# A planned Mamba and mixture-of-experts layer: ScalarE's side work cut into single activations, routing products into pieces, and new written-out orders

## The reference, cut to what matters

```python
xz = einsum('bld,ed->bel', x, in_proj_w);  x, z = halves           # 1024 channels each
x = silu(conv4(x) + conv_b)                                        # four taps along time
dt_lo, B, C = split(einsum('bdl,kd->blk', x, x_proj_w))
delta = softplus(dt_lo @ dt_proj_w.T + dt_proj_b)
h_t = h_(t-1) * exp(delta_t * A) + delta_t * B_t * x_t             # 16 states a channel
y = (sum over states of h * C + D * x) * silu(z);  out = y @ out_proj_w.T
x1 = layernorm(x + out)
w = softmax(top 2 of x1 @ gate_w.T)
x2 = layernorm(x1 + sum over the two experts of w * (x1 @ expert_w.T + expert_b))
```

## Time and profile before

| what | value |
|---|---|
| median of three runs | 2285.7 us (2283.76 to 2297.6) |
| span of the profiled execution | 2281.1 us |
| busy share of the span | PE 89%, DVE 87%, POOL 81%, ACT 73% |
| mean granted clock of PE | 0.941 of full speed |

### The profile page before, as it was taken

The page is one execution under the profiler, slowest core; times in us unless marked ns, Lnnn a source line. Parts: engine busy times, 40 slices in busy tenths (PEclk is TensorE's granted clock), DMA queues, the critical chain, the costliest instruction groups (busy, mean ns, idle before and its releaser), DMA issues.

```text
span 2281.1 us, 30428 instructions
## 1 busy us (share of the span) xinstructions
PE 2037.1 (89%) x8624; PEld 1201.8 (53%) x8624; DVE 1983.3 (87%) x2191; ACT 1660.2 (73%) x3074; POOL 1850.8 (81%) x1505
## 2 busy tenths in 40 slices
PE   8896779789898989999899989999799998879998
PEld 3444455455554645545555555645455555545543
DVE  5899999899999989898899899899898988889911
ACT  5758858677598856988588876989579785666534
POOL 2959999589898979889898889899898897686503
PEclk9896879889999999999999999999999999769999
DMA  5513143158854776557754687556855575466875
GB/s 169 180 47 92 38 139 111 51 172 252 278 129 143 241 255 180 143 168 257 256 152 119 201 266 234 129 180 216 284 149 141 180 252 209 123 209 215 278 278 120
DMA packets 222085, 412.79 MB, mean 181 GB/s; under 512 B 29880, under 2 KB 36152, under 8 KB 221920
## 3 DMA queue, kind: packets, MB, share of 16 engines
q1 hardware_dynamic: 180448, 322.36, 42.1%
q0 software_dynamic: 20496, 57.16, 12.3%
q10 hardware_dynamic: 20976, 31.33, 4.1%
HBM read 299.37 MB, written 85.72 MB: 169 GB/s over the span
## 4 chain that ended last, share of the span: by engine, by line
POOL 25%; PE 10%; issue 9%; DMA 7%; DVE 7%; ACT 3%; SPq 1%; ACTq 0%; DVEq 0%; POOLq 0%
POOL hst L1704 12%; PE bank L1137 8%; POOL first_dbu L1704 4%; DMA y<-scaled 2%; DVE hst L1755 2%; DVE y L1744 2%; POOL delta L1675 2%; POOL u L1678 2%; DVE hst L1920 1%; DMA Bbc<-b_scratch 1%; POOL ysb L1630 1%; DVE u L1775 1%; PE hTp L1153 1%; POOL zs L1649 1%; ACT dA L1563 1%
## 5 line engine op out<-in xcount | busy, mean ns | idle before, releaser
L1563 ACT ACTIVATE dA<-delta,negA 128x512 f32<-128x512 f32 (+1 forms) x1146 | 712.2, 636 | 307.9 <-DVE hst L1755 248.2
L1704 POOL TENSOR_TENSOR hst<-u,Bbc 128x512 f32<-128x512 f32 x666 | 870.7, 1412 | 42.3 <-PE hTp L1153 26.9
L1755 DVE TENSOR_TENSOR_SCAN hst<-dA,hst 128x512 f32<-128x512 f32 x672 | 791.0, 1211 | 50.9 <-ACT dA L1563 46.9
L1153 PEld LDWEIGHTS hTp<-ident,hst 128*128 128x128 f32 x4096 | 498.3, 149 | 325.6 <-issue 140.4
L1153 PE MATMUL hTp<-ident,hst 128*128 128x128 f32 x4096 | 560.1, 288 | 106.0 <-DVE hst L1755 33.7
L1744 DVE SCALAR_TENSOR_TENSOR y<-hTp,Ct,y 128x1024 f32<-128x1024 f32 x463 | 587.1, 1268 | 69.4 <-PE hTp L1153 54.9
L1704 POOL TENSOR_TENSOR first_dbu<-u,Bbc 128x512 f32<-128x512 f32 x222 | 292.9, 1393 | 42.0 <-DVE hits L1836 29.2
L1755 DVE TENSOR_TENSOR_SCAN hst<-dA,first_dbu 128x512 f32<-128x512 f32 x224 | 263.3, 1210 | 9.5 <-ACT dA L1563 7.0
L1137 PE MATMUL bank<-wslot,hidT 128*128 128x512 f32 x512 | 244.3, 610 | 10.4 <-ACT zs L1459 5.0
L1137 PE MATMUL bank<-wslot,tokT 128*128 128x512 f32 x480 | 234.6, 617 | 9.7 <-ACT tokT L1474 9.7
L1137 PE MATMUL bank<-delta,tokT 128*128 128x512 f32 x480 | 220.8, 593 | 0.0
(11 more groups left out here) (187 smaller groups left out, 2874.8 us busy)
## 6 DMA issues: line engine op xcount, KB each, us to landing
wslot<-in_w_expT SPq DMA_DIRECT2D x90, 1024.0 KB, 6.5
Bbc<-b_scratch SPq DMA_DIRECT2D x113, 256.0 KB, 3.5
wslot<-in_w_inT SPq DMA_DIRECT2D x26, 1024.0 KB, 6.1
y<-scaled POOLq DMA_DIRECT2D x49, 512.0 KB, 5.3
zs<-sorted_tokens ACTq DMA_DIRECT2D x91, 256.0 KB, 5.1
sorted_results<-ysb SPq DMA_DIRECT2D x90, 256.0 KB, 6.2
res<-in_w_expT SPq DMA_DIRECT2D x18, 1024.0 KB, 6.9
gate_scratch<-zs SPq DMA_DIRECT2D x64, 256.0 KB, 2.1
```

The source lines that it names most:

```text
L1153: mm = nc.tensor.transpose(hTp[q % 2][:, tok(j)], hst[n % 2][:, j, start:start + P], ident[:, :])
L1563: nc.scalar.activation(decay_of(step, halved), delta[w.odd][:, j, cols], ACT.Exp, scale=negA[:, j, n:n + 1]).then_inc(exp_done, 1)
L1704: nc.gpsimd.tensor_tensor(dbu_row(n, j), u[w.odd][:, j, :], Bbc[n % 2][:, :], ALU.mult).then_inc(dbu_done, 1)
L1755: nc.vector.tensor_tensor_scan(hst[n % 2][:, j, :], dA[j % 2][:, :], dbu_row(n, j), 0.0, ALU.mult, ALU.add).then_inc(scan_done, 1)
```

## The change

- `z`, `zb`, `sig` and `dt` are placed on ACT one activation at a time (`z`, `z1`, `z2`, `z3`, and so on); `ln` is cut into `rs` (three activations of one column each) and `ln` (one of 512).
- The `gate` product is four pieces and `count` two, where each was one block on PE.
- `plan()` knows the scaled parts: their cost on ACT and POOL, a landing 8 us after POOL's issue, and no addition on DVE. The seven scaled parts are now those of n = 0, 2, ... 12.
- Costs in `tasks()` and `start_main` are somewhat smaller, the tick is half as long.
- `stand_back` goes. `plan()` puts a `hold` into POOL's program behind the row that POOL has reached when DVE wants to start `gate`, `place` or `route`; POOL waits there for the same semaphore as before. SEG_EPI has none, before or after.
- In SEG_EPI `szE` and the two loads of the output weights (`WoE`) are issued by ACT.
- More than two turned pieces may stand behind the last part of a period; the expert tile `moe` 10 crosses into the next period only where it ends ACT's order; SP waits for `b_stored` ahead of a period's first B; a norm of SEG_LAST is cut but keeps its place.
- All bonuses and paces are new: pace 0.36 to 0.174 in SEG_PRO, 0.38 to 2.0 in SEG_TWO, 1.13 to 1.891 in SEG_FULL, 0.15 to 1.878 in SEG_EPI. So every order is new.

No instruction of the computation is added or left out.

```diff
-Z = [x for i in range(HALF * NT) for x in (("z", i), ("z2", i))]
+Z = [x for i in range(HALF * NT) for x in (("z", i), ("z1", i), ("z2", i), ("z3", i))]
...
-        own = [(x, "pe", 0.1), ((name + "2", k - 1), "act", 0), ((name, k - 2), "pool", 0.1), ((name, k - 2), "sp", 4)]
-        return [("pe", mm, before_pe + [((name + "2", k - 2), "act", 0), ((name, k - 3), "pool", 0)]), ("act", 1.25, own + before_act),
-                ("pool", 1.3, [((name + "2", k), "act", 0.1)]), ("sp", 0.5, [(x, "pool", 0.1)])]
+        own = [(x, "pe", 0.1), ((name + "3", k - 1), "act", 0), ((name, k - 2), "pool", 0.1), ((name, k - 2), "sp", 4)]
+        return [("pe", mm, before_pe + [((name + "3", k - 2), "act", 0), ((name, k - 3), "pool", 0)]), ("act", 0.52, own + before_act),
+                ("pool", 1.25, [((name + "3", k), "act", 0.1)]), ("sp", 0.5, [(x, "pool", 0.1)])]
...
-        "ln1": [("act", 1.5, [(("sq1", k), "act", 0.1)])],
+        "rs1": [("act", 0.95, [(("sq1", k), "act", 0.1)])],
+        "ln1": [("act", 0.85, [(("rs1", k), "act", 0.1)])],
...
-        "gate": [("pe", 3.0, [(("x1T", t), "act", 0.1) for t in range(NT)])] * (not alone)
+        "gate": [("pe", 0.9, [(("x1T", t), "act", 0.1) for t in range(NT)])] * (not alone)
...
-        "count": [("pe", 2.2, [(("gate",), "dve", 0.1)])],
+        "count": [("pe", 1.1, [(("gate",), "dve", 0.1)])],
...
-        "szE": [("sp", 0.5, [])],
+        "szE": [("act", 0.35, [])],
+        "WoE": [("act", 0.7, [])],
...
+        "z1": [("act", 0.52, [(("z", k), "act", 0)])],
+        "z2": [("act", 0.65, [(("z1", k), "act", 0)])],
+        "z3": [("act", 0.65, [(("z2", k), "act", 0.1)])],
...
+        "dt1": [("act", 0.7, [(("dt", k), "act", 0)])],
+        "dt2": [("act", 0.65, [(("dt1", k), "act", 0)])],
+        "dt3": [("act", 0.65, [(("dt2", k), "act", 0.1)])],
...
-SHARES = {"z": 4, "zb": 4, "x": 4, "out": 8, "moe": 4, "moeL": 4, "den": 4, "outF": 8, "xproj": 8}
+SHARES = {"z": 4, "zb": 4, "x": 4, "out": 8, "moe": 4, "moeL": 4, "den": 4, "outF": 8, "xproj": 8, "gate": 4, "count": 2, "countF": 2}
...
+           "z": ("z1", "act"), "zb": ("zb1", "act"), "moeL": ("moeL", "act"), "wT": ("wT", "act"), "moe": ("moe", "act"), "xproj": ("xproj", "act"), "dt": ("dt1", "act")}
...
+MAIN = ("exp", "dbu", "B", "part", "scan", "scaled", "landed")
+STILL = ("gate", "place", "route")
+TICK = 0.05
...
-BY_DMA = [NH * n + 2 for n in range(NS) if n % 2 == 1 and n < NS - 1]
+BY_DMA = [NH * n + 2 for n in range(NS) if n % 2 == 0 and n < NS - 2]
...
+    scaled_at = {} if halved else {2 * (q + NH + 1): q for q in BY_DMA}
...
+            return (r < 2 or ended(("scan", r - 2), "dve")) and (r not in scaled_at or ended(("part", scaled_at[r] + NH), "pe", 0.1))
...
+            return (r < 4 or ended(("scan", r - 4), "dve")) and (r - 5 not in scaled_at or ended(("scaled", scaled_at[r - 5]), "act", 0.1))
...
+        if r - ND in scaled_at and not ended(("landed", scaled_at[r - ND]), "pool"):
+            return False
+        return ended(("exp", r), "act", 0.1) and ended(("dbu", r), "pool", 0.1) and (r in scaled_at or r % 2 or r < 2 or ended(("part", r // 2 - 1), "pe", 0.15))
...
+        what, cost = {"act": (("exp", r), 0.65), "pool": (("dbu", r), 1.25), "sp": (("B", r), 0.5), "pe": (("part", r), 0.96),
+                      "dve": (("scan", r), (0.6 if halved else 1.12) + (1.2 if r in part_number and r not in scaled_at else 0))}[e]
...
+        if e == "act" and r in scaled_at:
+            free[e] += 1.05
+            done[("scaled", scaled_at[r]), e] = added[r] = free[e]
+        if e == "pool" and r - 5 in scaled_at:
+            free[e] += 1.0
+            done[("landed", scaled_at[r - 5]), e] = free[e] + 8
...
+            return added.get(row, 1e9) + 0.1 <= now and (len(here) < 2 or row == parts[-1] and ended(here[-2], "act", 0.1))
...
+            if e == "dve" and steps and not halved and x[0] in STILL:
+                if not hold:
+                    hold = x
+                    rows["pool"].append((row_of("pool"), ("hold",) + x, 0))
+                if free["pool"] > now + 1e-6:
+                    if steps and main_ready(e):
+                        tokens += pace
+                        start_main(e)
+                    continue
+                free["pool"] = now + cost + 0.1
+                hold = None
...
-SEG_FULL = Segment(by_urgency({"pp": -10390, "sk": -20915, "L0": 30876, "L1": -1699, "m0": -4874, "m1": -1377, "Zb": 8543, "py": -1361, "m2": -12569, "pd": -12545, "mb": -6204, "m3": 18895, "mw": -611, "ld": -12029, "o0": 5409, "o1": 12917, "ln": 9049, "sc": -52266, "lx": 10140, "px": 5525, "ps": -9849, "Za": -18093, "E0": -10085, "E1": -2724}), 1.13, W_FULL + W_O + GAP + [experts(2, LATE)], [x[0] for x in W_L])
+SEG_FULL = Segment(by_urgency({"pp": 44, "sk": -1043, "L0": 114, "L1": 385, "m0": 233, "m1": -155, "Zb": 289, "py": -129, "m2": 1094, "pd": -171, "mb": 2, "m3": -8, "mw": -196, "ld": 80, "o0": 294, "o1": 279, "ln": -57, "sc": -163, "lx": -13, "px": -163, "ps": 62, "Za": 268, "E0": -3, "E1": -1419}), 1.891, W_FULL + W_O + GAP + [experts(2, LATE)], [x[0] for x in W_L])
...
-                    pe.wait_ge(turned_taken, w.turn(("x1T", NT - 1))[2])
-                    for t in range(NT):
-                        mm = accumulate(ps[:, t * NE:(t + 1) * NE], lambda k: x1_turned(w, t)[:, tok(k)], lambda k: gate[:, k, :], KD)
+                    if share == 0:
+                        pe.wait_ge(turned_taken, w.turn(("x1T", NT - 1))[2])
+                    t = share
+                    mm = accumulate(ps[:, t * NE:(t + 1) * NE], lambda k: x1_turned(w, t)[:, tok(k)], lambda k: gate[:, k, :], KD)
...
-                    pe.wait_ge(hits_ready, w.e + 1 + w.tail)
-                    for t in range(NT):
-                        mm = nc.tensor.matmul(ps[:, NT * NE:(NT + 1) * NE], ones[:, :], hits[:, t, :], start=(t == 0), stop=(t == NT - 1))
-                    for i in range(NT):
-                        mm = nc.tensor.matmul(ps[:, i * NE:NT * NE], (ones if i else before)[:, :], hits[:, 0:NT - i, :],
-                                              start=(i == 0), stop=(i == NT - 1))
+                    if share == 0:
+                        pe.wait_ge(hits_ready, w.e + 1 + w.tail)
+                        for t in range(NT):
+                            mm = nc.tensor.matmul(ps[:, NT * NE:(NT + 1) * NE], ones[:, :], hits[:, t, :], start=(t == 0), stop=(t == NT - 1))
+                    else:
+                        for i in range(NT):
+                            mm = nc.tensor.matmul(ps[:, i * NE:NT * NE], (ones if i else before)[:, :], hits[:, 0:NT - i, :],
+                                                  start=(i == 0), stop=(i == NT - 1))
...
+                elif name in ("z1", "zb1"):
+                    i, (s, v) = x[1], w.bank((name[:-1], x[1]))
+                    ps = bank[s]
                     nc.scalar.activation(zs[i % 2][:, :], ps[:, :], ACT.Copy).then_inc(bank_taken[s], 1)
...
+                elif name == "szE":
+                    t = x[1]
+                    if t == 0:
+                        act.wait_ge(delta_ready, w.b * ND + ND)
+                        for k in range(2):
+                            act.wait_ge(z_stored[k], w.b * (16 * NT))
+                    elif t == PAIR:
+                        act.wait_ge(dbu_done, w.b * (NS * ND))
+                    act.dma_start(early_z(t, 0, HALF), z_dram[w.e, tok(t), :].rearrange("p (k n) -> p k n", k=HALF)).then_inc(early_in[t], 16)
+                elif name == "WoE":
+                    act.wait_ge(exp_done, w.b * (NS * ND))
+                    for h in range(HALF):
+                        s = w.weights(("Wo", h))[0]
+                        act.dma_start(slot_of(w, s), block_src(("Wo", h))).then_inc(w_loaded[s], 16)
...
-                    if step == 1 and w.b > 2 and w.seg.steps:
+                    if step == 1 and w.b > 2 and w.seg.steps and SEG_FULL.ends_with_tile:
...
+                elif x[0] == "hold":
+                    stand_still(w, x[1])
...
-                    if w.seg.steps and not w.seg.halved and step >= AHEAD:
-                        for x in w.seg.rows["dve"][step - AHEAD]:
-                            stand_back(w, x)
```

More of the change, by code:

```diff
@@ L35 @@
 BANKS = 2
-AHEAD = 2
 SLOTS = 17
@@ L283, in start_main @@
         main[e] += 1
-        what, cost = {"act": (("exp", r), 0.7), "pool": (("dbu", r), 1.3), "sp": (("B", r), 0.5), "pe": (("part", r), 1.05),
-                      "dve": (("scan", r), (0.6 if halved else 1.1) + (1.22 if r in part_number else 0))}[e]
+        what, cost = {"act": (("exp", r), 0.65), "pool": (("dbu", r), 1.25), "sp": (("B", r), 0.5), "pe": (("part", r), 0.96),
+                      "dve": (("scan", r), (0.6 if halved else 1.12) + (1.2 if r in part_number and r not in scaled_at else 0))}[e]
         if halved and e == "act":
             cost = 0.45
-        if e == "dve" and r in part_number:
-            added[r] = now + 1.22
```

(16 more changed lines are left out.)

149 lines of the change are left out of this document (80 added, 69 removed).

## The result

The changed kernel takes 2316.25 us (median of 4 runs, 2309.15 to 2323.27), the kernel before 2287.86 beside it: a ratio of 1.0134, with a 95% interval of 1.0096 to 1.0172. The forecast was 2239 us, its range ended at 2298.

A forecast was written before the change was run, and what follows sets the result against it. No engine alone was the bound; DVE's 176.6 us idle in the row stages was the target. Gains 38 + 10 + 3 + 10 + 4 + 6 = 71, less 24 coming back, gave 47 and 2239 us; own range 2191 to 2262, stated up to 2298.

The forecast's parts named there:

- New orders: DVE's waits for turned parts behind side products and each other, 50 us: 10 us gain, between 25 gained and 25 lost.
- slack of ACT: ACT's idle time in SEG_FULL, 1032.5 of 1312.3 us busy, was to hide the later side work.
- a stage whose side work no longer fits its 128 rows: Listed only as an unlisted way to be wrong: side work running behind the last scan; no size or chance given.
- Single activations: DVE's 57.8 us of waits for decays from ACT fall by two thirds, 38 us; ends nothing and 57.8.
- Transfers: DVE's 13.9 us of waits for scaled parts' transfers: 10 us gain, between 13.9 gained and 10 lost.
- Routing pieces: `gate` and `count` cut on PE let due turns come earlier: 3 us gain, between 0 and 13.
- The hold: POOL stands still where DVE is expected at routing steps: 4 us gain, between 14 gained and 16 lost.
- late hold: DVE's routing step runs beside POOL: 0.88 us lost per hold, 16 us at worst over 18.
- Loads of SEG_EPI: Gate values and output weights issued by ACT, starting earlier: 6 us gain, between 15 gained and 4 lost.
- What comes back: 35% of the 71 us gain returns as DVE's waits for PE and POOL, leaving 47 us.
- the 8.5 us of a period: The summed gain's share in one SEG_FULL period of 262.5 us, set against 24 us mean idle of PE and POOL.
- The late banks: Rival: Copy of `z` and Relu of `dt` return PSUM banks to PE later, 106 us delay, 2321 us; chance 0.11.

The follow-up runs named there:

- the base: The changed kernel with the five SEG_FULL periods in the written-out order of the kernel before: 2264.41 us, ratio 0.9907 to the kernel before.
- late8: Kernel of 2264.41 us (old SEG_FULL order, rest changed), every SEG_FULL piece from the fourth tile's norm on eight rows later, same sequence: 2333.92 us, ratio 1.0204.
- before_even: The kernel before with only the scaled parts moved to the change's even states: 2270.58 us, ratio 0.9944 to the kernel before.
- rejoined: The changed kernel, its rows kept, with ACT's single activations back in the runs of before: 2319.84 us, ratio 1.0141 to the kernel before.

## Why the prediction was wrong, point by point

**The step that failed** is "New orders", taken as 10 us of gain between 25 either way, and with it the cover named for all later side work, the "slack of ACT (1032.5 of 1312.3 us busy)". A mean share over five periods says nothing about the last 15 us of each. With the rest of the change kept, the new rows of SEG_FULL cost 52 us (2316 to 2264): 57.7 us of stand came behind the rows, which themselves took some 5 us less than the base's. The rows to look at were in the trace of before: the last expert tile ended 3 to 5 us ahead of the last scan, the `u` of the last `dt` 7 to 8 us ahead. An order that starts both chains some 15 us later, and shortens neither by as much, ends them 10 and 11 us past the last scan. That the order of SEG_FULL makes the stand is shown by the base; that lateness is the reason is shown by late8 for the old sequence and read from the rows in the new one. The prediction named this end ("a stage whose side work no longer fits its 128 rows") and gave it no chance and no price. The prediction weighed how much of each engine is idle, not when the chains end.

**Single activations, 38 us.** The number came true within the rows (20 us of waits left, as forecast), the reason did not: joined again the kernel is as fast, and placed singly by a row in the base it loses 56 us. What lowered the waits is the rows: those of SEG_FULL leave ACT's and POOL's pieces for the end, where they cost 57.7 us at the boundaries; and the states of the scaled parts, which take 14 us off the waits for decays in the kernel before (38.4 to 24.1).

**Transfers, 10 us.** Right in sign, too small: 13 us alone, 20 in the base. The plan's knowledge of the landing was not needed for it, since before_even has the old rows; whether the distance from the period's end did it is open. In the changed kernel the gain can't be seen (17.2 us of such waits, before 13.9).

**Routing pieces, 3 us.** Not tried by itself. In the changed kernel waits for turned parts fell from 53.2 to 35.3 us, but those for the bank of `res` rose from 8.9 to 32.5; PE's lateness moved.

**The hold, 4 us.** Right in sign; some 28 us in the new order, outside of the bounds of 14 and 16, and nothing in the old. A late hold, priced at 0.88 us each, did not occur: in the five periods `mix` took 163 to 165 ns, but POOL had nothing running within 0.3 us of it. In SEG_EPI of the changed kernel, where POOL ran beside it, it took 1.05 us, as the prediction's row had it, so that price stands.

**Loads of SEG_EPI, 6 us.** Not tried by themselves. SEG_EPI's two halves and SEG_LAST last 400.1 us before, 404.7 after, 399.1 in the base and 394.9 in before_even, which has the old loads and the old order there: no gain is seen. The first gate values were issued 2.6 us into the stage instead of 8.6, and the six issues took 5.04 us together, close to the bound of 5; the first half is 3.6 us longer all the same.

**What comes back, 24 us.** The share was taken from PE's and POOL's idle time, and the loss came from neither: it is chains that end behind the rows. The sum itself is off by little: 35% of 71 us is 25, not 24, and no row gives the 8.5 us of a period; 65 us, the 71 without SEG_EPI's loads, are 9.3 in each of seven. The late banks, the rival nearest in time (2321 us for 2316), were not its cause in the changed kernel, since rejoined takes as long.

## What to carry to other kernels

When side work is woven into a fixed main loop, find each dependent chain of it that has to end there and read two numbers from the trace, when it starts in the stage and how long it takes to its last piece; the sum against the end of the main loop is the slack, and a busy share is not. The length holds only for an order like the one it was read from. Where an instruction waits for two engines, compare when each of them was done, since the one that the profile names may have been done earlier. An order that lowers the waits within the rows may have paid for it behind the last one, so look at the longest wait of each row and not at its total alone. Take a bundle of changes apart early: here one line, the choice of the states, held most of the gain, and the kernel with the old rows of SEG_FULL and the rest of the change (2264 us) is faster than both.

## What the runs showed of the hardware that was not expected

A DMA issued by ACT took its queue 0.33 us where it was issued by itself, and up to 3.24 us in a row of nine within 11 us, at the start of SEG_EPI in the changed kernel:

```profile
1919.39 0.33 ACTq L1595 DMA_DIRECT2D hidT<-gate_scratch  x1
...
1926.88 3.24 ACTq L1613 DMA_DIRECT2D Bbc<-b_scratch  x1
...
1930.17 0.48 ACT L1638 ACTIVATE dA<-delta,negA 128x256 f32<-128x256 f32 x1 [1.76 <-issue]
```

The same load of B took 0.33 us to issue before (L1538 at 1890.63); after, the decay at 1930.17 stood 1.76 us with nothing but issues ahead of it. What in the row made the issues longer was not tried.

And the same 5327 products of SEG_FULL kept PE busy 1241.9 us after, at a mean granted clock of 0.95 of 2.4 GHz, and 1207.9 before, at 0.98; the clock goes between two levels, 1.2 and 2.4 GHz. In the period that starts at 828.3 it fell from 948 to 978 us (a mean of 0.83, with PE busy 26.0 of 30 us) and from 1008 to 1038 us (0.78), where the kernel before had 1.00 in the same stretches. What lowered it, and how much of the loss comes from it, was not settled.
